# A mixture-of-experts kernel: the copy of x and four transposes moved among the first expert's loads, and another order of work at both ends of each expert's first phase

## The reference

```python
# _L0_cond_ref: x is [8, 512, 512]
styles = w @ (affine_w * gain).T + affine_b
dcoefs = rsqrt(sum((weight[None] * styles[:, None])**2, axis=2) + 1e-8)
y = einsum('blc,oc->blo', x * styles[:, None], weight) * dcoefs[:, None]
y = clip(y + bias, -256, 256)
# _L0_ffn_ref: N = 4096 tokens, E = 8 experts, k = 1024 tokens each
scores = softmax(xt @ Wr, axis=-1)
G, idx = top_k(scores.T, k)
h = gelu(einsum('ekd,edh->ekh', xt[idx], W1) + b1)      # 512 -> 2048
X_e = einsum('ekh,ehd->ekd', h, W2) + b2                # 2048 -> 512
out = zeros.at[idx].add(G[..., None] * X_e)
return x + out
```

## Time and profile before

| | |
|---|---|
| time, median of 3 runs | 1599.72 us (1599.49 to 1600.64) |
| the profiled execution's own time | 1599.78 us |
| its span, first to last instruction | 1597.8 us |
| mean granted TensorE clock | 0.967 |
| PE busy | 1486.5 us, 93% of the span |
| DVE, ACT, POOL busy | 1005.6, 731.1, 186.7 us |
| DMA packets, data | 166204, 164.39 MB |

### The profile page before, as it was taken

The page is one execution under the profiler, slowest core; times in us unless marked ns, Lnnn a source line. Parts: engine busy times, 40 slices in busy tenths (PEclk is TensorE's granted clock), DMA queues, the critical chain, the costliest instruction groups (busy, mean ns, idle before and its releaser), DMA issues.

```text
span 1597.8 us, 18913 instructions
## 1 busy us (share of the span) xinstructions
PE 1486.5 (93%) x6759; PEld 1210.7 (76%) x6759; DVE 1005.6 (63%) x1687; ACT 731.1 (46%) x986; POOL 186.7 (12%) x158
## 2 busy tenths in 40 slices
PE   8993769999999999999999999999999999999995
PEld 6772547887878787887878787878788787878784
DVE  5667457767846676567647674668556764766432
ACT  6773335455445444463435444544445343544322
POOL 0001200221011200203010301130010201030003
PEclk9996879999999999999999999999999999999998
DMA  6874952474126430625144512543152514351014
GB/s 218 232 175 102 283 151 93 120 184 112 54 66 121 89 87 28 144 67 113 52 97 102 112 54 66 132 85 80 40 139 73 112 40 106 92 107 65 27 40 53
DMA packets 166204, 164.39 MB, mean 103 GB/s; under 512 B 109536, under 2 KB 109664, under 8 KB 165088
## 3 DMA queue, kind: packets, MB, share of 16 engines
q1 hardware_dynamic: 151632, 121.24, 27.7%
q0 software_dynamic: 14480, 41.95, 12.6%
HBM read 112.82 MB, written 33.55 MB: 92 GB/s over the span
## 4 chain that ended last, share of the span: by engine, by line
PE 82%; DVE 9%; issue 4%; SPq 2%; ACT 2%; DMA 1%; POOL 0%; POOLq 0%; DVEq 0%; ACTq 0%
PE Pt L1659 18%; PE BBt L1659 18%; PE Pt L1600 16%; PE BBt L1600 12%; PE BBt L1397 5%; PE BBt L1589 5%; PE Pt L1544 5%; SPq L437 2%; DVE OBx L1242 1%; DVE BBt L1219 1%; PE Pt L1428 1%; PE BBt L1409 1%; DVE RG L1201 1%; DVE RG L1195 1%; DVE RG L1235 1%
## 5 line engine op out<-in xcount | busy, mean ns | idle before, releaser
L1659 PE MATMUL Pt<-RG 128*128 128x512 f32 x1344 | 322.9, 389 | 0.0
L1659 PE MATMUL BBt<-RG 128*128 128x512 f32 x1344 | 322.8, 389 | 0.0
L1600 PE MATMUL Pt<-XT,RG 128*128 128x512 f32 x1176 | 295.1, 404 | 26.7 <-DVE PU L1210 26.7
L1659 PEld LDWEIGHTS Pt<-RG 128*128 128x128 f32 x1344 | 252.3, 188 | 52.5
L1659 PEld LDWEIGHTS BBt<-RG 128*128 128x128 f32 x1344 | 252.2, 188 | 52.4
L1600 PEld LDWEIGHTS Pt<-XT,RG 128*128 128x128 f32 x1176 | 229.2, 196 | 81.1 <-DVE PU L1210 32.2
L1600 PE MATMUL BBt<-XT,RG 128*128 128x512 f32 x1176 | 281.9, 390 | 8.2 <-DVE BBt L1219 8.2
L1600 PEld LDWEIGHTS BBt<-XT,RG 128*128 128x128 f32 x1176 | 219.7, 188 | 56.4 <-DVE BBt L1219 11.1
L1231 DVE TENSOR_TENSOR RG<-RAW,RG 128x512 fp32r<-128x512 f32 x112 | 77.7, 694 | 217.1 <-ACT RG L764 217.1
L764 ACT ACTIVATE RG<-RAW 128x512 fp32r<-128x512 f32 x112 | 70.6, 631 | 274.6 <-PE BBt L1659 271.0
L1235 DVE TENSOR_TENSOR RG<-H,RG 128x1024 fp32r<-128x1024 f32 x112 | 137.3, 1226 | 28.7 <-ACT RG L768 28.7
(11 more groups left out here) (223 smaller groups left out, 1554.6 us busy)
## 6 DMA issues: line engine op xcount, KB each, us to landing
RAW<-in_W SPq DMA_DIRECT2D x224, 256.0 KB
W1R<-in_W SPq DMA_DIRECT2D x32, 256.0 KB, 2.7
W2R<-in_W SPq DMA_DIRECT2D x32, 256.0 KB, 2.9
y_rows<-XR SPq DMA_DIRECT2D x32, 256.0 KB, 2.6
XB<-in_xT SPq DMA_DIRECT2D x7, 1024.0 KB, 6.9
B<-in_b SPq DMA_DIRECT2D x8, 256.0 KB, 8.0
WTraw<-in_WT SPq DMA_DIRECT2D x4, 256.0 KB, 6.9
XB<-in_xT SPq DMA_DIRECT2D x4, 256.0 KB, 7.5
```

What stands on the lines that cost most here:

```text
L1600: last = mm((Pt, BBt)[g % 2][:, bank, :], wslot(g)[:, a, w, 128 * k:128 * k + 128], XT[:, b, d, k, :], start=(begins and k == 0 and m == 0 ...
L1659: last = mm((Pt, BBt)[t // 4][:, t % 4, :], hslot(j)[:, a, hcol(t):hcol(t) + 128], w2slot(j)[:, d, :], start=(j == 0 and m == 0), stop=(j ...
```

## The change

Six places are edited. (1) On SP, the transposes 4 to 7 no longer stand ahead of the loads from W1 chunk 5 on, but each behind a pair of loads. (2) On POOL, the copy of x waits until all eight gathers of expert 0 have landed. (3) On VectorE, `build_rhs(e)` goes from step k = 1 of expert e - 1 to chunk 3 of the second phase before that, and for e = 2 to block 23 of expert 0. (4) `sums` and `lo_raw` of step 8n + 1 go behind u2 of step 8n. (5) On PE, P5 goes ahead of P7 in step 8n. (6) On PE, tile 0 of chunk 0 goes ahead of P3(8n + 7), the other tiles stay behind it.

```diff
             load_w1(3)
             load_w1(4)
-            for r in range(4, 8):
-                transposes(r)
             for i in range(3, NBLK):
                 if i + 2 < NBLK:
                     load_w1(i + 2)
                 load_w2(i)
+                if i < 7:
+                    transposes(i + 1)
...
+            for i in range(4):
+                eng.wait_ge(s_gat[i], 32)
             eng.dma_start(out.rearrange("(a b) d -> a (b d)", a=512),
                           x.rearrange("(a b) d -> a (b d)", a=512)).then_inc(s_o0, 16)
...
+                if i == 23:
+                    build_rhs(2)
...
             for t in range(4):
                 evac_second(t)
-            sums(1)
...
-                    if k < 7:
+                    if 0 < k < 7:
                         lo_raw(g + 1)
                     u2(g)
                     if k:
                         c12(g - 1)
+                    else:
+                        sums(g + 1)
+                        lo_raw(g + 1)
...
-                    if n + 2 < E:
-                        if k == 1:
-                            build_rhs(n + 2)
-                        if 1 <= k <= 4:
-                            build_oh(n + 2, k - 1)
+                    if n + 2 < E and 1 <= k <= 4:
+                        build_oh(n + 2, k - 1)
...
                     chunk_lo(16 * n + j)
+                    if n + 3 < E and j == 3:
+                        build_rhs(n + 3)
...
                 for t in range(4, 8):
                     evac(n, t)
-                if n + 1 < NX:
-                    sums(8 * n + 9)
...
-            def chunk(jj):
+            def chunk(jj, tiles):
...
-                for t in range(8):
+                for t in tiles:
...
-                if j < 15:
+                if j < 15 and t == 7:
                     last.then_inc(s_Bc, 1)
...
                     if k:
                         P3(g - 1)
+                    else:
+                        P5(g)
...
                     P7(g)
-                    P5(g)
+                    if k:
+                        P5(g)
...
+                chunk(16 * n, (0,))
                 P3(8 * n + 7)
-                for j in range(16):
-                    chunk(16 * n + j)
+                chunk(16 * n, range(1, 8))
+                for j in range(1, 16):
+                    chunk(16 * n + j, range(8))
```

## The result

The changed kernel's median is 1554.64 us in four executions, against 1599.87; the ratio is 0.970 (95% interval 0.964 to 0.976; it leaves the 1582.52 out). The forecast was 1547.5, in 1541 to 1556. But the four executions took 1582.52, 1561.15, 1548.13 and 1547.37 us. Two are on the forecast to a microsecond; the others are 14 and 35 us over it. The four of the kernel before had stayed within 1.2 us. A median of so few executions with such a spread says little by itself. The profile shown here is that of the 1582.52.

What follows compares the result with a forecast made beforehand. PE was taken as busy most of the span, so only its waits could be won: the expert 0 stall and each later expert's start. Gains 6.3 + 22.9 + 13.0 + 5.9 + 4.2 = 52.3 from 1599.8 gave 1547.5 us, range 1541 to 1556.

Steps and rivals of the forecast that it cites:

- First term, the queues: Expert 0: W1(5) and W2(3) land before the copy, PE gets one more block before stalling; gain 6.3 us.
- The rival for "slower": Start of each expert: VectorE's work moved behind u2 delays P1(8n+1); 1603 us at 8 us each, chance 0.02.
- Second term, u2 and P5: Start of experts 1 to 7: with u2 first and P5 before P7, P7 waits for nothing; gain 22.9 us.
- Third, the clock: Starts of six later experts: without the wait before P7 the clock no longer falls; gain 13.0 us.
- Fourth, build_rhs: Third step of six experts: u2 no longer late once build_rhs leaves the second step; gain 5.9 us.
- Fifth, tile 0: Before P3(8n+7): tile 0's three matmuls fill the wait for c22_c21; 0.6 us seven times, gain 4.2 us.
- The copy did not catch W1(5) or W2(3): Rival, expert 0: the copy catches one of these loads, PE stalls at 194.0; gain about 1, 1552.8 us, chance 0.12.
- Loads do not pass in one turn: Rival, expert 0: W1(6) and W2(4) also come through beside the copy, one more block runs; 1542.1 us, chance 0.10.
- No part of the waits for u2 stayed: Rival, expert starts: only P5's 1.36 us won each time, 1.96 remain; 1560 to 1573 us, chance 0.06.

Runs made afterwards that it cites:

- e3: The kernel before with only the SP and POOL edits (transposes among the loads, copy waiting for the gathers): 1591.38 shortest, 1631.31 median, 1665.53 us longest.
- e7: e4 with P5 behind P7 again in every step: median 1549.10 us, 8.3 over e4.
- e8: e4 with VectorE's earlier order at the start of an expert (sums and lo_raw ahead of u2; build_rhs stays moved): median 1557.61 us, 16.8 over e4.
- e11: The changed kernel with the copy in eight 1 MB pieces behind the transposes, but all tiles of chunk 0 behind P3(8n + 7) again: median 1532.82 us.
- e4: The changed kernel, but the copy of x waits until transposes 4 to 7 have landed, not only the gathers: median 1540.85 us.
- e10: The changed kernel with the copy in eight 1 MB pieces, one after the other, the first behind the gathers with transposes beside it: median 1530.53 us.
- e6: The changed kernel with the copy, behind the gathers, as eight DMAs of 1024 rows by 256 columns without waits between: median 1541.55 us.
- e12: The kernel before with only the VectorE and PE edits, plus the copy in eight pieces without a wait ahead of them: median 1535.60 us.

## Why the prediction was right, and where it was not

The measured median is in the range, but that is partly luck: 1554.64 is the middle of two executions without a jam and two with one. The sum is that of the executions without a jam (1545.0 to 1548.1 against 1547.5), and over all eleven executions of the kernel the middle one took 1561.15, outside the range.

*First term, the queues, 6.3 us.* The mechanism was right to the block: W1(5) and W2(3) through, W1(6) caught, the stall's begin at 199.1 against 199.8, shortest of e3 1591.4 against 1593.5. The step that failed is "the copy would be over about 208.3 to 208.9": it took the 28.6 us of one profile as a constant. With transposes in the queue beside it the copy took 43 to 66 us in the five profiles that show a jam, and the term is then a loss: 7 to 29 us in the six jammed executions of the changed kernel (against the 1553.8 of the other four terms), 24 to 66 us in the five of e3 (against the kernel before). The bounds set for it, 1 and 11.7, were on the moment at which the copy starts, none on its length. The earlier trace rows could have warned: there the two queues took turns one for one, so each small packet of a transpose already stood behind a 64 KB packet, and one profile says nothing of how that varies. The rival for "slower" was looked for on VectorE, which has no part in it.

*Second term, u2 and P5, 22.9 us:* right in mechanism, no wait for u2 is left; e7 and e8 show that it takes both halves. VectorE's lateness at step 8n + 1, bounded by 5.7, was nothing.

*Third, the clock, 13.0 us:* right, no fall in experts 1 to 7. It was worked out from three readings of each of two lengths by turns; all six in the trace of before are 8.34, 7.18, 8.30, 7.19, 8.36 and 7.17, which gives 12.9. PE's busy time for the same matmuls is 15.0 us less in the two windows above, some of it the modelled ends at waits.

*Fourth, build_rhs, 5.9 us:* right in mechanism, no wait is left at the third step, and none appeared where it went; no run has it alone, so its size isn't shown.

*Fifth, tile 0, 4.2 us:* mis-sized, 2.8 by e11. P3 waits 0.5 us as forecast. The step that was off is that 0.6 an expert is won at the BBt tiles of chunk 0 and kept. The rows of expert 1, e5 first, then e11:

```profile
435.28 2.97 PE L1665 MATMUL BBt<-RG 128*128 128x512 f32 x12
438.08 2.90 PE L1665 MATMUL Pt<-RG 128*128 128x512 f32 x12
```

```profile
436.90 2.88 PE L1665 MATMUL BBt<-RG 128*128 128x512 f32 x12
439.62 2.88 PE L1665 MATMUL Pt<-RG 128*128 128x512 f32 x12
```

Counted from the last two blocks of expert 0 (at 349.06 and 350.18), the BBt tiles come 0.50 us earlier in e5, and the Pt tiles of chunk 1 0.42 earlier: 0.1 is missing ahead of the first and 0.08 goes between the two. Some 0.4 an expert stay, as 2.7 / 7 says. What chunk 1 stands for in those 0.08 us isn't shown; I take it that it is the low half of H, which follows the same GELU.

Terms 2 to 5 came to 46.8 us against 46.0. As the fifth is 1.4 short, the other three together gave some 2 us more than forecast; which of them isn't known.

*The rivals.* The copy did not catch W1(5) or W2(3) in any profile. Loads do not pass in one turn (e4). No part of the waits for u2 stayed.

Beyond both kernels: e5, the changed order with the copy in eight pieces of 1 MB behind the transposes, takes 1530.04 us, 0.956 of before (0.954 to 0.958), and didn't jam in its five executions.

## What to carry to other kernels

This copy of 8 MB, issued as one DMA in rows of 16 KB, went out in packets of 64 KB on every engine, and each small packet of another queue waited for one of them: a 256 KB load beside it landed only when the copy was over. Look for such a copy in the list of DMA issues, and try it in pieces with a wait between them (e5, e10) before juggling what is ahead of it, with transposes kept out of its way. And when a term of a forecast rests on one profile's duration of a transfer beside others, give it a bound of its own and run the kernel more than three times.

## What of the hardware was not expected

DMA transposes (256-byte packets) beside a copy in 64 KB packets can bring the 16 engines nearly to a halt: 50 GB/s over 39 us against 336 GB/s with transposes beside the copy and no jam (183 to 222 of the changed kernel, 181 to 203 of the one before). It did not occur in 14 executions of e4, e7 and e8 (no transpose beside the copy), where the changed kernel had it in 6 of 11. With transposes beside it, it did not occur in 5 of e6 (4 KB packets) nor in 4 of e10 (pieces), though e10's first piece was held up too; the 5 of e12 say less, as the jam was rare in that order, and e5 and e11 have no transposes beside their pieces. That both transposes and a long row of 64 KB packets are needed is what these numbers speak for; why the engines wait for one another, and what decides whether an execution jams, stays open: that the engines are at unequal places in a transpose when the copy begins would fit the change having made it common, but no run tests it.
